# Folding a quarter of an adjacency tile onto another in TensorE, so that VectorE searches 6144 columns of a tile where it searched 8192

## The chip, the cores and the metric

The kernel runs on one core of a Trainium2 chip. The metric is device time in microseconds (us), the median of the runs. The engines are named as the profile names them: PE is TensorE (PEld its weight loads), DVE is VectorE, ACT is ScalarE, POOL is GpSimd, SP is SyncE, which here only issues DMAs.

## The reference, cut to what matters

One layer of graph attention over 8192 nodes with 256 features, 8 heads of 32, and a dense 8192 x 8192 adjacency matrix `adj` of which few entries are not zero: the probability of an entry falls with both its row and its column number, so the first rows and the first columns are the fullest (738 in the fullest row, and at most twenty in each of the last).

```python
h = relu(layernorm(x))
hw = (h @ W.T).reshape(n, H, D)                  # H = 8, D = 32
attn = s_src[:, None, :] + s_dst[None, :, :]     # s_src, s_dst: hw against a_src, a_dst
attn = attn + adj[:, :, None] * We[:, 0] + be
attn = where(adj[:, :, None] > 0, attn, -inf)
attn = softmax(leaky_relu(attn, 0.2), axis=1)
out = x + einsum('ijh,jhd->ihd', attn, hw) + h @ Wr.T + br
```

## The kernel before

Each row's few neighbours are found, their rows of a table are gathered, and attention is computed over the gathered rows alone.

The head (to 285 us) projects all nodes and writes a table of 8192 rows of 264 numbers (256 features, 8 scores) to DRAM; beside it the very full rows of tile 0 are searched in four "windows".

The loop has two streams. The first is the search. A tile is 128 rows of `adj`, 8192 columns, 4 MB. SP loads it in eight pieces of 1024 columns into one of two buffers (`adj_sb`); a piece of the tile after next waits until DVE has passed those columns (semaphore `scanned`). DVE cuts the columns into segments (the table `SEGS`: 35 for tile 1, 7 from tile 48 and 32 on) and takes from each segment the eight largest values of every row (`v.max`, L757) and their columns (`v.max_index`, L746), in `scan`. `keys` packs value and column into two words, `sort_step` sorts these with `max` and `match_replace`, `decode` writes a list of the K nearest columns and values of each row. If a segment holds eight or more entries in a row, the tile is flagged and would be computed densely at the end; so is one whose list is too short.

Tiles come in ten groups. When all tiles of a group are found, its rows are ranked by their number of neighbours, dealt to units by rank (POOL writes each row's list to its place in DRAM, `deal`, L625, and loads them back, `load_dealt`, L637), so that a unit is 128 rows with at most K neighbours. There are 67 units, K from 75 down to 7, and 1262 gathers in all.

The second stream is the units. For each, POOL issues K indirect DMAs (`gather`, L600), one for each neighbour number, into a ring of 86 slots; a gather waits until the gather four issues before it has landed (four lanes) and until PE has summed what stood in its slot. ACT prepares the scores, DVE does the softmax (L883 to L894), ACT the exponentials (L1166), DVE weights three fifths of the gathered rows (L904), ACT the rest (L1172), PE sums them in PSUM by matmuls with an identity (`tile_sums`, L1304 and L1310), and DVE scales the sum in the next unit (`evacuate`, L917). After the gathers of unit u, POOL stores unit u-4 by an indirect DMA (`store`, L616), which waits for that `evacuate`.

What sets the order: every engine has one program in order. DVE does in unit u the finds that the table `FOUND` gives it (19 in units 1 to 11, then one for each unit to unit 45, then 7 until unit 60), and the last of them is interleaved with the unit's softmax. PE has only `tile_sums` and a few small matmuls for ranks. The four windows' results are combined on DVE in units 60 to 63 and added to the output by POOL in unit 65 (L648).

## Time and profile before

| what | value |
|---|---|
| median of 3 runs | 2366.17 us (2361.86 to 2367.48) |
| the profiled execution | 2366.95 us, of which the trace spans 2365.2 |
| DVE busy | 2042.5 us, 86% |
| POOL busy | 1607.2 us, 68% |
| ACT busy | 1080.1 us, 46% |
| PE busy | 1011.7 us, 43%, mean granted clock 0.68 |

A busy share counts the time in which an engine executes. An engine that issues DMAs spends time around them too, which stands as idle time "ended by issue"; so POOL's 68% has to be read with the idle time in front of its instructions and with what ended it. Of the chain that ended last the page shows only the last DMA; who bounds the loop has to be read from the waits.

### The profile page before, as it was taken

The page shows a single profiled execution, that of the slowest core. Times are in us where ns is not written, and L with a number is a line of the kernel's source. Part 1 is how long each engine was busy: PE and PEld are TensorE (multiplying, and loading weights), DVE is VectorE, ACT ScalarE, POOL GpSimd, SP SyncE. Part 2 cuts the span into 40 slices and gives each one's busy share as a digit, 9 for nine tenths or more (in the row PEclk, how much of TensorE's full clock was granted, in tenths as well). Part 3 has the DMA queues.
Part 4 walks back from the last instruction along what each step waited for, and adds up shares of the span by engine and source line. Part 5 has one row for each costly group of instructions (what it writes and reads, how often), then busy time and mean ns, then how long its engine had stood idle before and what let it go on. Part 6 is the DMA issues. An engine that isn't in the chain of part 4 may idle for free. (4 is left out here: it accounts for less than half of the span.)

```text
span 2365.2 us, 22833 instructions
## 1 busy us (share of the span) xinstructions
PE 1011.7 (43%) x3773; PEld 798.4 (34%) x3774; DVE 2042.5 (86%) x5463; ACT 1080.1 (46%) x4646; POOL 1607.2 (68%) x1939
## 2 busy tenths in 40 slices
PE   4766304422453274336333543362344336353344
PEld 3555203322432153325322433252234225242232
DVE  4899798899699679998988899999999998888733
ACT  2333206532574264446544645453453446475454
POOL 5444476667676677667777777677677775677775
PEclk9988656666765566666666766676666666677676
DMA  6444876677676867787777688788888886777443
GB/s 145 158 144 139 298 211 167 196 232 229 138 210 216 233 165 223 233 247 213 238 230 227 190 254 254 236 244 255 254 259 245 258 263 189 207 215 207 99 89 67
DMA packets 167080, 489.46 MB, mean 207 GB/s; under 512 B 35888, under 2 KB 54360, under 8 KB 166728
## 3 DMA queue, kind: packets, MB, share of 16 engines
q1 hardware_dynamic: 86088, 278.11, 36.0%
q0 software_dynamic: 80848, 209.94, 34.5%
q14 instruction: 116, 0.95, 0.1%
q8 instruction: 28, 0.46, 0.1%
HBM read 451.08 MB, written 36.83 MB: 206 GB/s over the span
## 5 line engine op out<-in xcount | busy, mean ns | idle before, releaser
L600 POOL DMA_INDIRECT arena<-table,arena x1262 | 1285.7, 1019 | 504.3 <-issue 316.3
L1304 PE MATMUL banks<-arena,ident 128*128 128x264 f32 x1566 | 501.8, 493 | 1206.3 <-DVE arena L904 1206.3
L1304 PEld LDWEIGHTS banks<-arena,ident 128*128 128x128 f32 x1566 | 386.2, 252 | 1319.0 <-issue 1092.4
L1172 ACT ACTIVATE arena<-arena 128x32 f32<-128x32 f32 x3832 | 819.3, 306 | 2.2
L746 DVE FIND_INDEX8 work<-work,adj_sb 128x8 uint32<-128x502 f32 (+56 forms) x775 | 667.0, 865 | 0.0
L757 DVE MAX8 work<-adj_sb 128x8 f32<-128x502 f32 (+56 forms) x775 | 652.1, 856 | 0.0
L1166 ACT ACTIVATE arena<-pre 128x104 f32<-128x104 f32 (+22 forms) x81 | 23.2, 302 | 998.2 <-DVE pre L894 998.2
L1310 PE MATMUL banks<-arena,ident 128*128 128x264 f32 x958 | 253.8, 407 | 39.2 <-ACT arena L1172 38.8
L904 DVE TENSOR_TENSOR arena<-arena 128x1024 f32<-128x1024 f32 (+8 forms) x169 | 226.3, 1388 | 37.4 <-ACT arena L1166 37.3
L1310 PEld LDWEIGHTS banks<-arena,ident 128*128 128x128 f32 x958 | 181.7, 196 | 99.4 <-ACT arena L1172 71.9
L1156 ACT ACTIVATE pre<-arena,we_all 128x13 f32<-128x13 f32 (+26 forms) x536 | 165.2, 406 | 87.7 <-DMA arena<-lists 87.7
L883 DVE TENSOR_TENSOR pre<-pre,arena 128x104 f32<-128x104 f32 (+22 forms) x81 | 21.5, 280 | 187.6 <-DMA arena<-table,arena 76.4
L806 DVE MAX8 work<-work 128x8 f32<-128x56 f32 (+11 forms) x580 | 132.9, 270 | 2.3
L808 DVE MATCH_REPLACE8 work<-work 128x56 f32<-128x56 f32 (+11 forms) x446 | 118.3, 272 | 0.2 <-issue 0.2
L616 POOL DMA_INDIRECT out_dram<-w_all,arena x41 | 66.7, 1626 | 47.1 <-DVE w_all L917 23.4
L1114 ACT ACTIVATE arena<-arena 128x256 f32<-128x256 f32 x64 | 29.0, 500 | 146.5 <-DVE arena L712 146.4
L625 POOL DMA_INDIRECT lists<-arena,rank x67 | 66.9, 999 | 36.5 <-issue 21.3
L1280 PE MATMUL banks<-w_all,arena 128*128 128x272 f32 x256 | 83.5, 455 | 1.9 <-ACT arena L1122 1.8
L1326 PE MATMUL banks<-work,ones 128*128 128x24 f32 (+9 forms) x390 | 80.2, 356 | 0.0
L1326 PEld LDWEIGHTS banks<-work,ones 128*128 128x128 f32 x390 | 75.9, 287 | 0.0
L570 POOL TENSOR_TENSOR arena<-arena 128x512 f32<-128x512 f32 x32 | 40.4, 1263 | 48.7 <-DVE arena L727 48.5
L1283 PE MATMUL banks<-w_all,arena 128*128 128x256 f32 x256 | 72.8, 411 | 0.0
(127 smaller groups left out, 931.8 us busy)
## 6 DMA issues: line engine op xcount, KB each, us to landing
adj_sb<-in_adj_dram SPq DMA_DIRECT2D x505, 512.0 KB, 4.6
arena<-table,arena POOLq DMA_INDIRECT x1262, 4.0
table<-arena POOLq DMA_DIRECT2D x32, 264.0 KB, 2.6
arena<-in_x_dram SPq DMA_DIRECT2D x32, 256.0 KB, 2.9
resid<-arena POOLq DMA_DIRECT2D x32, 256.0 KB, 2.6
out_dram<-arena POOLq DMA_DIRECT2D x32, 256.0 KB, 2.8
adj_sb<-in_adj_dram SPq DMA_DIRECT2D x1, 1536.0 KB, 23.1
lists<-arena,rank POOLq DMA_INDIRECT x67, 3.8
```

The lines of the kernel that those rows point to most:

```text
L600: pool.indirect_dma_start(gath[:, un.slot(k), :], None, table[:, :], bass.IndirectOffsetOnAxis(ap=rec[:, k, 0:1], axis=0)).then_inc(lane, 16)
L746: v.max_index(idx8[:, 8 * s:8 * s + 8], val8[:, 8 * s:8 * s + 8], a[:, bounds[s]:bounds[s + 1]]).then_inc(S["scanned"], 1)
L757: v.max(val8[:, 8 * s:8 * s + 8], a[:, bounds[s]:bounds[s + 1]]).then_inc(S["maxed"], 1)
L806: v.max(top, keys_of).then_inc(done, 1)
L808: v.match_replace(keys_of, top, keys_of, 0.0).then_inc(done, 1)
L904: last = v.tensor_tensor(gv, gv, pb.unsqueeze(3).to_broadcast([P, n, H, D]), ALU.mult)
L1156: last = s.activation(pv[:, h, :], pairs(rec, K)[:, :, 1], ACT.Identity, scale=we_all[:, h:h + 1], bias=rec[:, 1 + h:2 + h])
L1172: last = s.activation(g, g, ACT.Copy, scale=gath[:, un.slot(k), HD + h:HD + h + 1])
L1280: m.matmul(ps_hd[:, q, b, :], rows, w_all[:, c, 0:272], start=(c == 0), stop=(c == 1))
L1304: last = m.matmul(ps_sum[:, u % 2, :], ident[:, :], gath[:, un.slot(k), :], start=(k == 0), stop=False)
L1310: last = m.matmul(ps_sum[:, u % 2, :], ident[:, :], gath[:, un.slot(k), :], start=False, stop=(k == K - 1))
L1326: m.matmul(rv[:, i, :], ones[:, :], same[:, j * D:(j + 1) * D], start=False, stop=(i == n - 1 and j == i - 1))
```

## The change

From tile 5 on (59 of 63 tiles) PE adds, for four banks of PSUM of 512 columns each, columns 4096 to 6143 of the tile (times an identity) and columns 6144 to 8191 (times an identity scaled by 2^-64). A bank holds then both halves: what stands near keeps its size (0.05 to 1), what stands far is below 2^-32. DVE searches the four banks as four segments and columns 0 to 4095 in 5 to 11 more. `unfold` then marks the small values, adds the distance to their column and multiplies them by 2^64. Two entries of one row that fall on the same folded column, or eight of a row in a bank, would flag the tile; the table `TURNS` turns the far banks against the near ones, tile by tile. To tell a collision, ACT counts the entries of both halves (two `Sign` activations of 2048 columns with an accumulator, `see_fold`), DVE counts those found, and `fold_flags` compares the counts at the end. The pieces of a folded tile are loaded upper half first, and the upper half's buffer is free when ACT has counted it (`fold_seen`). The table `SEGS` is another, and `FOUND` ends the finds at unit 57 where it was 60.

The diff, cut to its core (semaphore names, bases of the segments and buffers are left out; of the tables the lines that the text speaks of stand):

```diff
+FOLD_FROM = 5
+FOLD_SCALE = 2.0 ** -64
-FOUND = ((0, 7), (11, 26), (45, 60), (60, 67))
+FOUND = ((0, 7), (11, 26), (45, 60), (57, 67))
...
-                for n in range(PIECES):
+                for i, n in enumerate(so.pieces):
                     cols = slice(n * PIECE, (n + 1) * PIECE)
-                    lane = S[f"adj_in{b}{n % 2}"]
-                    sp.wait_ge(S["scanned"], segs_before[c - 2] + scans_of(sources[c - 2], n))
+                    lane = S[f"adj_in{b}{i % 2}"]
+                    if sources[c - 2].folded and n * PIECE >= FOLD_AT:
+                        sp.wait_ge(S["fold_seen"], sources[c - 2].fold + 1)
+                    else:
+                        sp.wait_ge(S["scanned"], segs_before[c - 2] + scans_of(sources[c - 2], n))
...
+                def segment(s):
+                    if s < so.banks:
+                        return ps_fold[:, s, :]
+                    return a[:, bounds[s - so.banks]:bounds[s - so.banks + 1]]
...
+                    elif s < so.banks:
+                        dve.wait_ge(S["folded"], BANKS * so.fold + s + 1)
...
+            def unfold(so):
+                f = so.fold
+                vf, jf = val8[:, 0:8 * BANKS], jpad[:, 0:8 * BANKS]
+                v.tensor_scalar(fold_tag[:, :], vf, FOLD_SPLIT, 1.0 / FOLD_SCALE, ALU.is_lt, ALU.mult
+                                ).then_inc(S["tagged"], 1)
+                v.tensor_scalar(fold_one[:, 0, :], vf, FOLD_SPLIT, 0.0, ALU.is_ge, ALU.add,
+                                accum_out=fold_found[:, 0, f:f + 1])
+                v.tensor_scalar(fold_one[:, 1, :], vf, 0.0, 0.0, ALU.is_gt, ALU.add,
+                                accum_out=fold_found[:, 1, f:f + 1])
+                dve.wait_ge(S["jshift"], so.c + 1)
+                dve.wait_ge(S["tagged"], f + 1)
+                cut = 8 * (BANKS - so.turn)
+                for lo, hi, far in ((0, cut, FOLD + BANK * so.turn), (cut, 8 * BANKS, BANK * so.turn)):
+                    if hi > lo:
+                        last = v.scalar_tensor_tensor(out=jf[:, lo:hi], in0=fold_tag[:, lo:hi],
+                                                      scalar=float(far << JBITS) * FOLD_SCALE, in1=jf[:, lo:hi],
+                                                      op0=ALU.mult, op1=ALU.add)
+                v.scalar_tensor_tensor(out=vf, in0=fold_tag[:, :], scalar=1.0, in1=vf, op0=ALU.max, op1=ALU.mult
+                                       ).then_inc(S["unfolded"], 1)
+                dve.wait_ge(S["unfolded"], f + 1)
...
+            def see_fold(so):
+                act.wait_ge(S["folded"], BANKS * (so.fold + 1))
+                for side in range(2):
+                    cols = adj_sb[:, so.buf, FOLD_AT + FOLD * side:FOLD_AT + FOLD * (side + 1)]
+                    last = s.activation(cols, cols, ACT.Sign, bias=tiny[:, :],
+                                        accum_out=fold_counts[:, side, so.fold:so.fold + 1])
+                last.then_inc(S["fold_seen"], 1)
...
+                while seen < found[un.u]:
+                    if sources[seen].folded:
+                        see_fold(sources[seen])
+                    seen += 1
                 exps(un)
...
+            def fold(so):
+                before = sources[so.c - 1]
+                for q in range(BANKS):
+                    near, far = FOLD_AT + BANK * q, FOLD_AT + FOLD + BANK * ((q + so.turn) % BANKS)
+                    adj_landed(pe, so, near, near + BANK)
+                    adj_landed(pe, so, far, far + BANK)
+                    if before.folded:
+                        pe.wait_ge(S["scanned"], segs_before[before.c] + q + 1)
+                    m.matmul(ps_fold[:, q, :], ident[:, :], adj_sb[:, so.buf, near:near + BANK], start=True, stop=False)
+                    m.matmul(ps_fold[:, q, :], small_ident[:, :], adj_sb[:, so.buf, far:far + BANK], start=False, stop=True
+                             ).then_inc(S["folded"], 1)
...
             for un in units:
+                while folds < min(len(sources), found[un.u] + 1):
+                    if sources[folds].folded:
+                        fold(sources[folds])
+                    folds += 1
                 tile_sums(un)
```

DVE, the end of the search of one late tile and its keys, in the kernel before (`flag` and the 128x56 words are the seven segments' results):

```order
L746 MAX_INDEX work<-work,adj_sb 128x8
L757 MAX work<-adj_sb 128x8
L746 MAX_INDEX work<-work,adj_sb 128x8 x3
L769 TENSOR_REDUCE flag<-work 128x1
L772 SCALAR_TENSOR_TENSOR work<-work,seg_base_20 128x56
L776 SCALAR_TENSOR_TENSOR work<-work 128x56
L780 SCALAR_TENSOR_TENSOR work<-work 128x56
L782 SCALAR_TENSOR_TENSOR work<-work 128x56
```

The same place on DVE in the changed kernel, whose nine segments are four banks and five pieces of the lower half:

```order
L800 MAX work<-adj_sb 128x8
L791 MAX_INDEX work<-work,adj_sb 128x8 x3
L857 TENSOR_REDUCE flag<-work 128x1
L860 SCALAR_TENSOR_TENSOR work<-work,seg_base_5_17 128x72
L811 TENSOR_SCALAR fold_tag<-work 128x32
L813 TENSOR_SCALAR fold_one,fold_found<-work 128x32
L815 TENSOR_SCALAR fold_one,fold_found<-work 128x32
L822 SCALAR_TENSOR_TENSOR work<-fold_tag,work 128x32
L825 SCALAR_TENSOR_TENSOR work<-fold_tag,work 128x32
L866 SCALAR_TENSOR_TENSOR work<-work 128x72
L870 SCALAR_TENSOR_TENSOR work<-work 128x72
L872 SCALAR_TENSOR_TENSOR work<-work 128x72
```

Five instructions of 32 columns stand between the first and the second instruction on the keys, and the words are 72 wide where they were 56.

PE, the sums of three units (K of 18, 17 and 15) in the kernel before, where `ident` is the identity and `banks` is PSUM:

```order
L1304 MATMUL banks<-arena,ident 128x264 x11
L1310 MATMUL banks<-arena,ident 128x264 x7
L1304 MATMUL banks<-arena,ident 128x264 x11
L1310 MATMUL banks<-arena,ident 128x264 x6
L1304 MATMUL banks<-arena,ident 128x264 x9
L1310 MATMUL banks<-arena,ident 128x264 x6
```

PE at the first two of these in the changed kernel, with the fold of one tile between them:

```order
L1411 MATMUL banks<-arena,ident 128x264 x11
L1417 MATMUL banks<-arena,ident 128x264 x7
L1447 MATMUL banks<-adj_sb,ident 128x512
L1448 MATMUL banks<-adj_sb,small_ident 128x512
L1447 MATMUL banks<-adj_sb,ident 128x512
L1448 MATMUL banks<-adj_sb,small_ident 128x512
L1447 MATMUL banks<-adj_sb,ident 128x512
L1448 MATMUL banks<-adj_sb,small_ident 128x512
L1447 MATMUL banks<-adj_sb,ident 128x512
L1448 MATMUL banks<-adj_sb,small_ident 128x512
L1411 MATMUL banks<-arena,ident 128x264 x11
L1417 MATMUL banks<-arena,ident 128x264 x6
```

Eight matmuls of 512 columns have come in front of each unit's sums; they are those of the tile that is searched one unit later.

POOL, the end of the program in the kernel before, with the deal (`lists`) and the load (`arena<-lists`) of the last group:

```order
L600 DMA arena<-table,arena 128x264 x11
L616 DMA out_dram<-w_all,arena 8192x256
L600 DMA arena<-table,arena 128x264 x9
L616 DMA out_dram<-w_all,arena 8192x256
L600 DMA arena<-table,arena 128x264 x8
L616 DMA out_dram<-more_out,arena 8192x256
L625 DMA lists<-arena,rank 512x45 x4
L637 DMA arena<-lists 128x4x45
L600 DMA arena<-table,arena 128x264 x18
```

The same units on POOL in the changed kernel (L686 adds the windows' combined result):

```order
L638 DMA arena<-table,arena 128x264 x11
L654 DMA out_dram<-w_all,arena 8192x256
L663 DMA lists<-arena,rank 512x45 x4
L638 DMA arena<-table,arena 128x264 x9
L654 DMA out_dram<-w_all,arena 8192x256
L675 DMA arena<-lists 128x4x45
L638 DMA arena<-table,arena 128x264 x8
L654 DMA out_dram<-more_out,arena 8192x256
L686 DMA out_dram<-adj_sb 128x256
L638 DMA arena<-table,arena 128x264 x18
```

The deal stands two units earlier and the load one unit earlier; between the deal, the load and the gathers that use them there are now other gathers. The gathers and stores are the same ones in the same order.

## Rows read from the trace of the kernel before

**Rows 1.** Page, part 1: busy us (share of the span) xinstructions

```profile
PE 1011.7 (43%) x3773; PEld 798.4 (34%) x3774; DVE 2042.5 (86%) x5463; ACT 1080.1 (46%) x4646; POOL 1607.2 (68%) x1939
```

**Rows 2.** Groups by line, POOL: busy us, mean ns | idle us before <-who ended it

```profile
L600 POOL DMA_INDIRECT arena<-table,arena x1262 | 1285.7, 1019 | 504.3 <-issue 316.3 <-DMA arena<-table,arena 134.7 <-DMA arena<-lists 27.5
...
L616 POOL DMA_INDIRECT out_dram<-w_all,arena x41 | 66.7, 1626 | 47.1 <-DVE w_all L917 23.4 <-DMA arena<-table,arena 20.0 <-issue 3.7
...
L543 POOL MEMSET seg_base<- 128x8 f32 x155 | 5.4, 95 | 0.0
```

**Rows 3.** Waits, all engines: engine line <- whom: us, times, longest us

```profile
DVE pre L883 <- DMA arena<-table,arena: 76.4, 14, 11.5
...
POOL arena L600 <- PE banks L1304: 1.8, 3, 1.2
```

**Rows 4.** POOL's timeline, its first gather: start us, us, instruction [idle before <-who]

```profile
284.88 1.01 POOL L600 DMA_INDIRECT arena<-table,arena  x1 [7.59 <-DMA arena<-lists]
```

**Rows 5.** POOL's timeline around unit 48's end

```profile
1979.19 0.95 POOL L600 DMA_INDIRECT arena<-table,arena  x1 [0.30 <-issue]
1994.22 1.62 POOL L616 DMA_INDIRECT out_dram<-w_all,arena  x1 [14.08 <-DVE w_all L917]
```

**Rows 6.** POOL's timeline at the last group's lists

```profile
2264.76 0.81 POOL L637 DMA_DIRECT2D arena<-lists  x1 [1.51 <-DMA lists<-arena,rank]
2268.07 1.00 POOL L600 DMA_INDIRECT arena<-table,arena  x1 [2.51 <-DMA arena<-lists]
```

**Rows 7.** Timeline of all engines at the end

```profile
2340.23 0.22 DVE L883 TENSOR_TENSOR pre<-pre,arena 128x56 f32<-128x56 f32 x1 [7.98 <-DMA arena<-table,arena]
...
2342.38 4.72 PE L1304 MATMUL banks<-arena,ident 128*128 128x264 f32 x10 [4.40 <-DVE arena L904]
...
2349.07 1.56 POOL L616 DMA_INDIRECT out_dram<-w_all,arena  x1 [3.46 <-DVE w_all L917]
```

**Rows 8.** Waits of POOL from 400 to 1000 us

```profile
POOL arena L600 <- DMA arena<-table,arena: 51.7, 81, 2.5
```

**Rows 9.** Waits of POOL from 1400 to 2000 us

```profile
POOL arena L600 <- DMA arena<-table,arena: 37.3, 59, 1.7
POOL out_dram L616 <- DVE w_all L917: 20.0, 2, 14.1
```

**Rows 10.** Waits of POOL from 2000 us to the end

```profile
POOL arena L600 <- DMA arena<-table,arena: 9.6, 20, 1.5
```

**Rows 11.** Stretches: busy us of each engine, granted clock, DMA share, GB/s

```profile
600.00:800.00 200.00, 91.71 (x324) 66.48 (x324) 177.41 (x480) 118.28 (x541) 138.62 (x135) 0.67 0.69 199
1600.00:1800.00 200.00, 83.81 (x298) 68.35 (x298) 197.74 (x425) 89.76 (x393) 144.49 (x141) 0.64 0.83 256
```

**Rows 12.** Groups by line and shape, DVE's search and sort

```profile
L746 DVE FIND_INDEX8 work<-work,adj_sb 128x8 uint32<-128x2173 f32 x16 | 38.6, 2415 | 0.0
...
L806 DVE MAX8 work<-work 128x8 f32<-128x56 f32 x192 | 31.8, 206 | 1.1
...
L806 DVE MAX8 work<-work 128x8 f32<-128x72 f32 x128 | 23.3, 223 | 0.5
...
L746 DVE FIND_INDEX8 work<-work,adj_sb 128x8 uint32<-128x502 f32 x16 | 10.8, 675 | 0.0
```

**Rows 13.** DVE's timeline, the key words of one tile

```profile
1604.78 0.22 DVE L780 SCALAR_TENSOR_TENSOR work<-work 128x56 uint32<-128x56 uint32 x1
1604.91 0.21 DVE L782 SCALAR_TENSOR_TENSOR work<-work 128x56 uint32<-128x56 uint32 x1
```

**Rows 14.** Groups by line, DVE, two from SBUF alone and with PSUM

```profile
L847 DVE TENSOR_TENSOR work<-degree,work 128x192 f32<-128x192 f32 (+9 forms) x11 | 4.0, 361 | 0.4
...
L859 DVE TENSOR_TENSOR work<-work,banks 128x192 f32<-128x192 f32 (+9 forms) x11 | 3.8, 348 | 3.4 <-PE banks L1328 3.4
```

**Rows 15.** Groups by line, ACT

```profile
L1172 ACT ACTIVATE arena<-arena 128x32 f32<-128x32 f32 x3832 | 819.3, 306 | 2.2
...
L1114 ACT ACTIVATE arena<-arena 128x256 f32<-128x256 f32 x64 | 29.0, 500 | 146.5 <-DVE arena L712 146.4
```

More of the change, by code:

```diff
@@ L102, in __init__, with base, places @@
             self.shape = SEGS[max(a for a in SEGS if a <= t)]
-            self.bounds, self.exact = segments(*self.shape), 0
+            self.bounds, self.exact = segments(*self.shape, FOLD_AT if t >= FOLD_FROM else N), 0
             self.buf, self.col = c % 2, 0
-        self.segs = len(self.bounds) - 1
+        self.folded = t is not None and t >= FOLD_FROM
+        self.banks = BANKS if self.folded else 0
+        self.turn = TURNS[t - FOLD_FROM] if self.folded else 0
+        self.fold = t - FOLD_FROM if self.folded else None
+        self.segs = self.banks + len(self.bounds) - 1
+        self.pieces = [(n + (PIECES // 2 if self.folded else 0)) % PIECES for n in range(PIECES)]
+    def base(self):
+        return [FOLD_AT + BANK * q for q in range(self.banks)] + list(self.bounds[:-1])
+    def places(self, cols):
+        return [i for i, n in enumerate(self.pieces) if cols[0] < (n + 1) * PIECE and cols[1] > n * PIECE]
     def windows(self):
@@ L198, in plan, with segments @@
     return sources, units, groups, found, issued
-def segments(n, power):
+def segments(n, power, width):
     bounds = [0]
     for s in range(1, n + 1):
-        bounds.append(max(bounds[-1] + 8, int(round(N * (s / n) ** power))))
+        bounds.append(max(bounds[-1] + 8, int(round(width * (s / n) ** power))))
     return bounds
@@ L237, in gat_kernel @@
         ps_out = banks[:, 4:6, 256:256 + D]
+        ps_fold = banks[:, 4:4 + BANKS, :]
         ps_rank, ps_above = banks[:, 2, :], banks[:, 3, :]
@@ L247, in gat_kernel @@
         we_all = sb("we_all", [P, H])
-        seg_base = {(n, w): sb(f"seg_base{n}_{int(10 * w)}", [P, n * 8]) for n, w in sorted(set(SEGS.values()))}
+        seg_base = {(f, n, w): sb(f"seg_base{f}_{n}_{int(10 * w)}", [P, (f + n) * 8])
+                    for f, n, w in sorted({(so.banks,) + so.shape for so in sources[NV:]})}
         s_all = sb("s_all", [P, TILES, H])
@@ L422, in scans_of, with adj_landed @@
         def scans_of(so, n):
-            return sum(lo < (n + 1) * PIECE for lo in so.bounds[:-1])
+            return so.banks + sum(lo < (n + 1) * PIECE for lo in so.bounds[:-1])
+        def adj_landed(eng, so, *cols):
+            for i in so.places(cols)[-2:]:
+                eng.wait_ge(S[f"adj_in{so.buf}{i % 2}"], 16 * (loads_before(so) * (PIECES // 2) + i // 2 + 1))
         def loads_before(so):
@@ L539, in _ @@
             pool.memset(adj_sb[:, 0, :], 0.0).then_inc(S["window_zero"], 1)
-            for (n, power), base in seg_base.items():
-                bounds = segments(n, power)
-                for s in range(n):
-                    last = pool.memset(base[:, 8 * s:8 * s + 8], float((bounds[s] + PAD) << JBITS))
+            for shape, base in seg_base.items():
+                so = next(so for so in sources[NV:] if (so.banks,) + so.shape == shape)
+                for s, at in enumerate(so.base()):
+                    last = pool.memset(base[:, 8 * s:8 * s + 8], float((at + PAD) << JBITS))
             for so in sources[:NV]:
@@ L751, in scan @@
                         dve.wait_ge(S[f"window_in{c}"], 16 * sum(1 for _ in so.windows()))
-                    else:
-                        pieces, before = -(-bounds[s + 1] // PIECE), loads_before(so)
-                        for lane in range(2):
-                            if pieces > lane:
-                                dve.wait_ge(S[f"adj_in{b}{lane}"], 16 * (before * (PIECES // 2) + (pieces - lane + 1) // 2))
-                    v.max(val8[:, 8 * s:8 * s + 8], a[:, bounds[s]:bounds[s + 1]]).then_inc(S["maxed"], 1)
+                    elif s < so.banks:
+                        dve.wait_ge(S["folded"], BANKS * so.fold + s + 1)
+                    else:
+                        adj_landed(dve, so, 0, bounds[s - so.banks + 1])
+                    v.max(val8[:, 8 * s:8 * s + 8], segment(s)).then_inc(S["maxed"], 1)
                     if s >= 2:
@@ L774, in keys @@
                                        ).then_inc(S["jshift"], 1)
+                if so.folded:
+                    unfold(so)
                 dve.wait_ge(S["jshift"], c + 1)
```

63 lines of the change are left out of this document (54 added, 9 removed).

## The prediction

> **What bounds the kernel now.** The page's busy shares come first [rows 1]: DVE 86%, POOL 68%, ACT 46%. By these DVE is the bound, and the change takes work from DVE. The waits say otherwise, so I read them second, POOL's first.
>
> POOL's gathers are one instruction group [rows 2]: 1262 of them, 1285.7 us busy and 504.3 us idle in front of them, together 1790.0 us. They begin at 284.88 us [rows 4]. The timeline shows how one costs: 0.95 us of execution and 0.30 us in front of it that waits for nobody [rows 5], so 1.25 us each even when everything is there. Of the 504.3 us idle, "issue" holds 316.3, the landing of earlier gathers 134.7, lists 27.5 [rows 2]; the wait for a ring slot, that is for PE's sums, is 1.8 us in the whole run [rows 3]. Add the stores, deals and loads on the same queue, and POOL is occupied from 285 us to the end with next to no wait for another compute engine. The exception is the store of unit u-4, which waited for DVE's `evacuate`: 23.4 us in all [rows 2], of which 20.0 in two waits between 1400 and 2000 us [rows 9], one of them 14.08 us long [rows 5].
>
> DVE, the busiest by the page, waits for POOL: 76.4 us for gathers in front of the softmax [rows 3]. The last unit shows the pair plainly: DVE idles 7.98 us until the gather has landed at 2340 us, and nine microseconds later all is stored but the last result [rows 7]. So the loop has two nearly equal streams. Between about 1400 and 2000 us DVE is the slower one (197.7 of 200 us busy, [rows 11]), POOL runs ahead until it hits the store, and elsewhere POOL sets the pace. Only what DVE makes POOL wait for can be won.
>
> **The change part by part.**
>
> *DVE's search.* FIND_INDEX8 takes 2415 ns for 2173 columns and 675 for 502 [rows 12], so 1.041 ns a column; MAX8 stands within 11 ns of it. 2048 columns less, searched twice: 2048 x 2 x 1.041 = 4.26 us a tile, times 59 = 251.6 us removed. The segments of all tiles rise from 624 to 700 (both tables summed over the tiles and windows). A segment's fixed part is 675 - 502 x 1.041 = 152 ns for one pass, of which the neighbours overlap some; between 0.1 and 0.3 us for both passes, I take 0.19: 76 x 0.19 = 14 us added. A late tile sorts 72 words for 56: 223 against 206 ns [rows 12], 17 ns on 15 instructions in some 32 tiles, 8 us.
>
> *`unfold`.* Five instructions, six in the 12 tiles that are turned: 307. The trace has short ones of the same kind at 0.13 us from start to start and 0.21 to 0.22 us each [rows 13]; 307 x 0.13 = 40 us to 307 x 0.25 = 77 us (the upper with a wait), I take 58. DVE's sum is -251.6 + 14 + 8 + 58 = -172 us, 8% of its busy time.
>
> PE writes the banks that DVE reads, and reading PSUM is no dearer here: 348 ns for an operation that reads PSUM against 361 for its twin from SBUF [rows 14]. The Trainium skill, "VectorE: DVE Perf Modes", section on the TRN2 errata, gives 120 cycles of fixed cost from PSUM and 58 from SBUF at 0.96 GHz; that would be an estimated 65 ns on 8 scans of 59 tiles, 30 us, and DVE's saving 142 us. The trace does not agree with it.
>
> *PE.* 8 matmuls of 512 columns a tile. Ten of 264 took 4.72 us [rows 7], 0.47 each; by columns 0.92 for 512, 7.3 us a tile and 431 us in all, bounded by nothing if all is hidden and by 7.3 us a tile if none is. A tile's fold stands one unit ahead of its search, in front of that unit's sums, which wait for DVE's weights of the same unit, after a whole search. PE is busy 84 of 200 us [rows 11]. Hidden, with slack: POOL's ring does not wait for PE [rows 3].
>
> *ACT.* 306 ns for 32 columns and 500 for 256 [rows 15] give 0.87 ns a column; 2048 columns 2.05 us, two of them 4.1 us a tile, 242 us in all. They stand in front of the unit's exponentials, which wait for DVE's search anyway; ACT is busy 90 to 118 of 200 us [rows 11]. Hidden. If that cover goes, DVE's weighting is late by up to 4.1 us a unit.
>
> *New waits.* DVE's first four scans wait for `folded`; queued behind are the softmax and `evacuate`, for which POOL's stores wait, with about a unit (20 us) to spare. SP's upper pieces wait for ACT's count and not for DVE's scan, so they come as a burst of four; the gathers on POOL meet them on the way.
>
> *Where it reaches the end.* The two store waits of 20.0 us go (but for 0.30 in front of each): -19.4. If DVE should remain slower there, nothing goes; if other POOL waits were DVE's as well, the bound is the 23.4 of [rows 2]. What is late next is POOL itself, gather after gather. The last group's deal moves two units up and its load one, past other gathers: its waits of 1.51 and 2.51 us [rows 6] fall to 0.30 each, -3.4, or stay. The head gets 49 more small memsets on POOL (204 for 155), whose 155 took 5.4 us [rows 2]: +1.7 on DVE's start. The earlier end of the finds (unit 57) only moves DVE's work.
>
> *The landing waits.* 134.7 us over 2055 us of loop is 0.066 a microsecond. From 400 to 1000 us it is 51.7/600 = 0.086 [rows 8], from 2000 us on, with the finds thinning out, 9.6/366 = 0.026 [rows 10]. At the one rate throughout the loop they would be 177 us (+42), at the other 54 (-81). The bytes are the same and the time nearly so; I take 0, since the rate between 1400 and 2000 us, 37.3/600 = 0.062 [rows 9], is no higher although the DMA share is (0.83 against 0.69, [rows 11]).
>
> Sum: 2366.95 - 19.4 - 3.4 + 1.7 = 2345.9 us for the profiled execution, which is 0.8 above the median shown; so 2345 us.
>
> **The rivals.**
>
> *DVE is the bound after all.* Then its whole 172 us come out: 2366 - 172 = 2194 us. For it: 86% busy, and near 99% from 1600 to 1800 us. Against it: POOL's gathers alone, at 1.25 us, are 1578 us, and POOL waits for DVE only 23 us. A part of it, 40 us or more gained, would need the landing waits to fall as well.
>
> *Nothing moves.* The 20 us come back as landing waits elsewhere, since POOL is then one steady stream and its DMA lanes never rest: 2360 to 2371 us. For it: in [rows 8] each such wait is 0.64 us (51.7 in 81), and 33 more of them are enough.
>
> *The loads collide with the gathers (slower).* The place is the four lanes of POOL in units 1 to 45, where every find issues four upper pieces at once and ACT's count, not DVE's scan, sets their moment. If the landing waits rise by more than 21 us, 16% of 134.7, the gain is gone. At the highest rate of the rows the time is 2345 + 42 = 2387 us; with the waits doubled, 2345 + 135 = 2480. Against it: the rate does not follow the DMA share. The Trainium skill, "Trainium Kernel Development and Optimization", Key Constraints, says that DMAs issued by SP, ACT and POOL run on the same 16 DMA engines and interleave; by that a burst must lengthen the gathers beside it, and what it adds would have to come back when the queue is empty.
>
> *The search waits for its fold (slower).* In units with two finds the second tile's fold stands behind the sums of the unit before, and these end with ACT's share of the weighting (K of 20 to 75). If 15 us a unit showed in 11 units, 165 us, and POOL's lead hid half, the time would be some 2345 + 80 = 2425 us.
>
> *The change doesn't do what it says*: a collision of two entries would flag a tile and bring the dense path. With these inputs the folded banks hold at most 7 entries in a row and no two on one column, worked out from the reference's inputs; no chance.
>
> **How the numbers follow.** Forecast (20 us gained, between 8 and 60) 0.55; DVE the bound, wholly or in part, over 60 us gained, 0.09; nothing moves 0.18; loads collide 0.13; the search waits 0.05. A difference under 0.3% (7 us) can't be told from none. Faster 0.55 + 0.09 = 0.64, same 0.18, slower 0.18. The range of 8 in 10 runs from 2300 us, which takes in landing waits 45 us shorter (half of that bound), to 2390 us, the collision at the highest rate of the rows.
>
> **What would show it.** DVE about 1870 us busy, its wait in front of the softmax up by some 150 us, POOL's store waits for DVE gone, POOL's gathers as before at 1.25 us from start to start, PE up by 430 us, ACT by 240, no wait of 0.5 us or more for `folded`. I am wrong if POOL's landing waits differ by more than 20 us from 134.7, if the ring makes POOL wait for PE, or if gathers get shorter than 0.95 us.

## The result and the profile after

The changed kernel takes 2379.33 us (median of 4 runs, 2376.05 to 2380.1) against 2365.95 for the kernel before in the same comparison: a ratio of 1.0058 (95% interval 1.0043 to 1.0073). It is slower by 13.4 us where 20 us less was forecast. The profiled execution has a span of 2377.9 us and a time of 2379.56 us.

The work came and went as it was meant to. The page's first part, busy us of each engine, against [rows 1]:

```profile
PE 1435.4 (60%) x4717; PEld 982.6 (41%) x4718; DVE 1865.6 (78%) x6123; ACT 1314.5 (55%) x4882; POOL 1606.0 (68%) x1989
```

DVE has 176.9 us less, PE 423.7 more, ACT 234.4 more, and POOL, which sets the pace, is unchanged. So the time must be in POOL's pauses. Its groups by line (busy us, mean ns | idle us before, and who ended it), against [rows 2]:

```profile
L638 POOL DMA_INDIRECT arena<-table,arena x1262 | 1281.9, 1016 | 547.5 <-issue 299.0 <-DMA arena<-table,arena 191.5 <-DMA arena<-lists 17.0
...
L654 POOL DMA_INDIRECT out_dram<-w_all,arena x41 | 66.4, 1619 | 21.1 <-DMA arena<-table,arena 10.9 <-issue 5.4 <-DVE w_all L1007 4.1
```

The idle time before the stores fell from 47.1 to 21.1 us, and DVE's part in it from 23.4 to 4.1: the forecast's gain is there. But the idle time before the gathers rose from 504.3 to 547.5 us, and within it the waits for landings from 134.7 to 191.5. (Each such wait contains the 0.30 us that stands before every gather, and "issue" shrank by 17.3 us as more gathers waited; so the net price is the 43.2 us.) From the first gather to the last is 2066.3 us, 13.3 more than before; that is the whole result. Counted from the records over this whole stretch, each wait less the 0.30 us that stands before every DMA on this queue: POOL's waits for landings of its own transfers (gathers, stores, deals) rose from 117 to 160 us, its waits for DVE fell from 19 to 0, its waits for lists from 24 to 13. That is +43 - 19 - 11 = +13 us. The head is no part of it: the first gather starts 1.5 us earlier than in [rows 4].

```profile
283.37 1.01 POOL L638 DMA_INDIRECT arena<-table,arena  x1 [4.68 <-DMA arena<-lists]
```

By stage, POOL's waits from 400 to 1000, 1400 to 2000 and 2000 us on, in this order, against 51.7, 37.3 and 9.6 in [rows 8 to 10]:

```profile
POOL arena L638 <- DMA arena<-table,arena: 59.6, 73, 2.7
```
```profile
POOL arena L638 <- DMA arena<-table,arena: 57.5, 79, 2.5
```
```profile
POOL arena L638 <- DMA arena<-table,arena: 23.4, 35, 1.9
...
POOL out_dram L654 <- DVE w_all L1007: 4.1, 1, 4.1
```

The rise is largest in the stretch that held the two store waits, 20 us; from 2000 us on, where the finds thin out, it is still 14. The only wait of a store for DVE that is left there is that of the last unit. POOL's timeline shows how a landing wait looks: the second gather here needs the lane of the one four before it, and that had not landed for another 2.02 us.

```profile
1618.06 0.95 POOL L638 DMA_INDIRECT arena<-table,arena  x1 [0.30 <-issue]
1621.02 0.95 POOL L638 DMA_INDIRECT arena<-table,arena  x1 [2.02 <-DMA arena<-table,arena]
```

DVE now waits for POOL, in front of the softmax 179.2 us against 76.4 in [rows 3]; and its search waits for the fold:

```profile
DVE pre L973 <- DMA arena<-table,arena: 179.2, 23, 16.8
DVE pre L973 <- DMA part_ml<-ml,arena: 76.8, 2, 51.6
...
DVE work L800 <- PE banks L1448: 47.8, 32, 17.8
```

What released the loads has changed too. SP's waits, first in the kernel before, then after (L486 and L523 issue a tile's pieces, L485 and L522 wait for the piece two before):

```profile
SPq L486 <- DVE work L746: 1135.9, 277, 47.4
SPq L485 <- DMA adj_sb<-in_adj_dram: 608.3, 344, 7.0
```
```profile
SPq L522 <- DMA adj_sb<-in_adj_dram: 904.2, 378, 7.1
SPq L523 <- ACT adj_sb L1272: 720.9, 49, 104.3
...
SPq L523 <- DVE work L791: 91.8, 28, 32.8
```

Before, 277 waits for DVE's scan metered the pieces out one by one. Now SP waits 49 times, about once a tile, for ACT's count, 28 times for DVE, and else for its own landings: from the count on, the pieces go out nearly as fast as the two lanes take them. A load is in flight from its issue until it has landed. Counted from the records of all loads, two or more were in flight for 42% of the gather loop before and 55% after, exactly one for 29% and 8%. From the records of gathers, the mean time from the end of the issuing instruction to the landing is 2.05 us beside no load, 3.0 before and 2.8 after beside one, and 4.0 beside two in both kernels; beside three, which only the changed kernel has (24 gathers), it is 5.5. Three more gathers at 1.25 us and the 0.30 us give some 4.05 us before a lane is wanted again, so two loads are the point at which four lanes begin not to suffice.

### The profile page after: what moved, and what is told of

The parts are those of the page before. It is cut to its first block and busy times, and to the rows that moved or that the text cites. A ratio compares the mean times of both kernels' runs of the same rounds, so it can differ in the third digit from the quotient of the medians.

```text
span 2377.9 us, 25865 instructions
## 1 busy us (share of the span) xinstructions
PE 1435.4 (60%) x4717; PEld 982.6 (41%) x4718; DVE 1865.6 (78%) x6123; ACT 1314.5 (55%) x4882; POOL 1606.0 (68%) x1989
## 5 line engine op out<-in xcount | busy, mean ns | idle before, releaser
L638 POOL DMA_INDIRECT arena<-table,arena x1262 | 1281.9, 1016 | 547.5 <-issue 299.0
L791 DVE FIND_INDEX8 work<-work,adj_sb 128x8 uint32<-128x266 f32 (+44 forms) x615 | 392.4, 644 | 0.0
L800 DVE MAX8 work<-adj_sb 128x8 f32<-128x266 f32 (+44 forms) x615 | 388.2, 633 | 0.0
L1447 PE MATMUL banks<-adj_sb,ident 128*128 128x512 f32 x472 | 266.9, 649 | 101.4 <-DMA adj_sb<-in_adj_dram 93.0
L973 DVE TENSOR_TENSOR pre<-pre,arena 128x104 f32<-128x104 f32 (+22 forms) x81 | 21.9, 284 | 363.6 <-DMA arena<-table,arena 179.2
L1448 PE MATMUL banks<-adj_sb,small_ident 128*128 128x512 f32 x472 | 256.1, 626 | 0.0
L1272 ACT ACTIVATE adj_sb<-adj_sb,tiny 128x2048 f32<-128x2048 f32 x118 | 234.4, 1987 | 31.3 <-PE banks L1448 31.3
L800 DVE MAX8 work<-banks 128x8 f32<-128x512 f32 x236 | 153.5, 686 | 47.9 <-PE banks L1448 47.8
L791 DVE FIND_INDEX8 work<-work,banks 128x8 uint32<-128x512 f32 x236 | 163.0, 691 | 0.0
L1448 PEld LDWEIGHTS banks<-adj_sb,small_ident 128*128 128x128 f32 x472 | 96.6, 205 | 127.4 <-issue 127.4
L896 DVE MAX8 work<-work 128x8 f32<-128x72 f32 (+14 forms) x580 | 136.7, 277 | 2.3
L898 DVE MATCH_REPLACE8 work<-work 128x72 f32<-128x72 f32 (+14 forms) x446 | 120.6, 278 | 0.0
```

The lines of the kernel that those rows point to most:

```text
L638: pool.indirect_dma_start(gath[:, un.slot(k), :], None, table[:, :], bass.IndirectOffsetOnAxis(ap=rec[:, k, 0:1], axis=0)).then_inc(lane, 16)
L791: v.max_index(idx8[:, 8 * s:8 * s + 8], val8[:, 8 * s:8 * s + 8], segment(s)).then_inc(S["scanned"], 1)
L800: v.max(val8[:, 8 * s:8 * s + 8], segment(s)).then_inc(S["maxed"], 1)
L896: v.max(top, keys_of).then_inc(done, 1)
L1272: last = s.activation(cols, cols, ACT.Sign, bias=tiny[:, :], accum_out=fold_counts[:, side, so.fold:so.fold + 1])
L1447: m.matmul(ps_fold[:, q, :], ident[:, :], adj_sb[:, so.buf, near:near + BANK], start=True, stop=False)
```

## The experiments

Each ratio is to the kernel before, run beside it; the changed kernel's is 1.0058. "Landing" is POOL's wait of gathers for gathers (134.7 us before, 191.5 after). "Lanes" is the count from above over all of POOL's waits for landings of its own transfers in the gather loop, each less 0.30 us (117 before, 160 after). The edits below are cut to the lines that matter, and shortened within the line.

| run | time us | ratio, 95% interval | landing us | lanes us | DVE busy us |
|---|---|---|---|---|---|
| e2 count early | 2392.24 | 1.0109 [1.0082, 1.0135] | 195.9 | 169 | 1862 |
| e3 after, 6 lanes | 2278.63 | 0.9641 [0.9616, 0.9666] | 51.4 | 24 | 1863 |
| e4 before, 6 lanes | 2316.08 | 0.9789 [0.9768, 0.9811] | 52.5 | 27 | 2046 |
| e5 before, less search | 2381.85 | 1.0086 [1.0066, 1.0106] | 161.6 | 148 | 1852 |
| e6 before, bunched | 2369.72 | 1.0044 [1.0025, 1.0063] | 160.7 | 145 | 2044 |
| e7 after, half pieces | 2350.59 | 0.9954 [0.9935, 0.9972] | 99.4 | 70 | 1873 |
| e8 after, 8 lanes | 2219.40 | 0.9402 [0.9384, 0.9420] | 32.6 | 4 | 1867 |
| e9 before, 8 lanes | 2312.88 | 0.9779 [0.9763, 0.9796] | 40.7 | 16 | 2048 |
| e10 before, e5 + e6 | 2402.57 | 1.0148 [1.0123, 1.0172] | 177.2 | 172 | 1853 |
| e11 after, more search | 2386.23 | 1.0082 [1.0064, 1.0101] | 188.3 | 162 | 2035 |
| e12 after, small count | 2394.93 | 1.0115 [1.0083, 1.0148] | 192.7 | 174 | 1864 |
| e13 after, spread | 2390.78 | 1.0110 [1.0081, 1.0139] | 198.7 | 165 | 1865 |
| e14 after, spread, more search | 2383.37 | 1.0081 [1.0052, 1.0110] | 172.6 | 156 | 2034 |
| e15 after, paced by the scan | 2365.72 | 1.0014 [0.9994, 1.0034] | 179.8 | 147 | 1864 |
| e16 = e15, more search | 2364.26 | 1.0002 [0.9985, 1.0020] | 175.6 | 136 | 2035 |

### Half of the change, in the kernel before

**e1, a shorter search (no verdict).** The segments of tiles 8 and on span 6656 columns instead of 8192.

```
-self.bounds = segments(*self.shape)
+self.bounds = segments(*self.shape, N if t < 8 else SHORT)
```

> The kernel before, with DVE searching only columns 0 to 6655 of each tile from tile 8 on (56 tiles; all 8192 columns are still loaded, the output lacks the neighbours left out). DVE loses about 2 x 1536 x 1.041 ns x 56 = 179 us of work, as the change does (177 us measured), with no fold on PE, no count on ACT and the loads released by DVE's scan as before. Theory A (the change's late and bunched release of the loads lengthens the gathers): the 20 us of store waits go, POOL's landing waits stay near 135 us, 2345 us (ratio 0.991). Theory B (POOL without pauses takes back in landing waits whatever DVE gives): landing waits 155 us or more, 2366 us or above.

It took 9399 us: rescaled segments hold eight entries of a row, tiles are flagged, and the dense path runs (PE has 16,125 matmuls instead of 3773). It says nothing of the question; e5 takes its place.

**e5, a shorter search.** The segments stay as they are and are clipped at 6656 columns, from tile 5 on; the entries beyond are left out.

```
+self.bounds = clipped(segments(*self.shape), N if t < 5 else SHORT)
```

> The kernel before, with DVE searching only columns 0 to 6655 from tile 5 on, its segments cut off there (all columns are still loaded; the neighbours in the last 1536 columns are left out, the 1262 gathers stay). DVE loses 2 x 1536 x 1.041 ns x 59 = 189 us of work; PE, ACT and the rule by which DVE's scan releases the loads are as before. Theory A (what lengthens the gathers is how the change bunches its loads): store waits gone, landing waits near 135 us, 2340 to 2350 us. Theory B (any time that DVE gives back is lost again in landing waits): landing waits 155 us or more and 2360 us or above.

DVE lost 190 us, the stores' waits for DVE went, as in the changed kernel, and the kernel became slower by 0.9%, as theory B had it. Its gathers' row shows where:

```profile
L606 POOL DMA_INDIRECT arena<-table,arena x1262 | 1287.5, 1020 | 524.0 <-issue 307.1 <-DMA arena<-table,arena 161.6 <-DMA arena<-lists 21.5
```

Not quite "all loads as before": the last two pieces, beyond the clip, are now released together, so there is some bunching in it (two or more loads in flight for 48% of the loop instead of 42%, one for 20% instead of 29%).

**e6, the loads in a bunch.** All eight pieces of a tile wait for the whole scan of the tile two back.

```
-sp.wait_ge(S["scanned"], segs_before[c - 2] + scans_of(sources[c - 2], n))
+sp.wait_ge(S["scanned"], segs_before[c - 2] + sources[c - 2].segs)
```

> The kernel before, with all eight pieces of a tile released together when DVE has passed the whole tile before last, and nothing else changed. Theory A: two loads are in flight for more of the loop, landing waits rise from 135 us to 170 to 200, and the time to 2385 to 2410 us. Theory B: DVE works as before, so landing waits and time stay (2366 us), unless DVE has to wait for columns, which the trace would show in front of its MAX8.

With DVE's work unchanged (2044 us) the landing waits rise by 26 us and the time by 0.4%; two or more loads are in flight for 55% of the loop. The sign is theory A's, the size is not: it expected 170 us or more of landing waits and 2385 us or more. POOL, slower by its lanes, also waits less for DVE at the stores of `w_all` (8.5 us, 23.4 before), which pays a part of the price.

**e10, both at once.**

> The kernel before with both halves of the cause: segments clipped at 6656 columns from tile 5 on (entries beyond are left out, DVE does some 189 us less), and a tile's eight pieces released together once the tile two back is scanned. If the two causes add up, landing waits 134.7 + 27 + 26, about 188 us, and 2385 to 2400 us. If either alone makes the whole effect (both only let POOL run without pauses), about 162 us of landing waits and 2375 to 2383 us.

2402.57 us: in time the two add up (0.9 + 0.4 against 1.5%), and in the lanes nearly (31 + 28 against 56 us). In the landing waits alone they do not quite: 42.5 against 53 us.

### Taking away what the waits are made of

**e3 and e4, six gather lanes.** The same edit in the changed kernel and in the one before.

```
-LANES = 4
+LANES = 6
```

> The changed kernel with six lanes for POOL's indirect DMAs (a gather waits for the landing of the gather six before, not four). If landing waits are what the change lost its gain to, and are waits for a lane and not a full DMA queue: landing waits from 191 us to under 40, POOL's loop 2066 us less about 140, 2230 to 2260 us. If the DMA queue itself is full, gathers get longer than 1.0 us instead and the time stays within 20 us of 2379.

> The kernel before with six lanes. The landing waits of 135 us go as in the changed kernel, but DVE (2042 us busy) then sets the pace for more of the loop: store waits on DVE rise from 23 us to 60 or more, 2300 to 2330 us, so that the changed kernel with six lanes is 2 to 4% faster than this one. If the DMA queue itself is full: 2366 us.

The landing waits fall to 51 and 52 us in both, most of which is the 0.30 us that each contains (119 and 117 waits), and both kernels get faster. In e4 DVE then holds up the stores. e3 missed its expectation (under 40 us and 2230 to 2260 us), and so the change is worth 1.5% at six lanes (0.9641 / 0.9789), not 2 to 4. e3 has an odd end: its last store is issued at 2215.0 us, and what follows takes 64 us, where every other run here but e1 takes some 16; without those 48 us the change would be worth 3.7%.

**e9 and e8, eight lanes.** The same edit with 8, before and after.

> The kernel before with eight gather lanes for four. Theory B (with lanes to spare the landing waits go, and then DVE's work is what counts): as with six lanes, 2316 +- 8 us, since DVE is the bound by then; POOL's store waits for DVE stay near 65 us, gathers wait under 5 us for landings. With the changed kernel's 2219 us at eight lanes the change is then worth about 4%. Theory A (the change costs time whatever the lanes are): about 2219 / 1.006, that is 2206 us.

> The changed kernel with eight lanes for POOL's indirect DMAs. With six the waits in front of the gathers beyond 0.30 us are already down to some 45 us, of which half are for lists and stores: another 10 to 25 us less, 2255 to 2270 us, if the lanes are all that holds POOL. If the DMA queue is full, gathers get longer and the time stays at 2279 us.

The kernel before gains nothing more over six lanes; the changed one reaches 2219 us, the fastest here, and below its expectation, which was reckoned from e3 with its long end. Against each other that is 0.9402 / 0.9779 = 0.961: with lanes to spare the change is worth 3.9%. POOL's stores in e9, and then its gathers and stores in e8:

```profile
L616 POOL DMA_INDIRECT out_dram<-w_all,arena x41 | 67.3, 1641 | 76.8 <-DVE w_all L917 65.2 <-issue 10.1 <-DMA arena<-table,arena 1.5
```
```profile
L638 POOL DMA_INDIRECT arena<-table,arena x1262 | 1280.2, 1014 | 411.9 <-issue 355.4 <-DMA arena<-table,arena 32.6 <-DMA arena<-lists 11.9
L654 POOL DMA_INDIRECT out_dram<-w_all,arena x41 | 68.1, 1662 | 18.1 <-issue 10.7 <-DVE w_all L1007 6.9 <-DMA arena<-table,arena 0.6
```

411.9 us before 1262 gathers is 0.33 each, near the 0.30 of an unhindered one. In e9 the stores wait 65 us for DVE, in e8 they wait 7.

**e7, pieces of half the size.**

```
-PIECES = 8
+PIECES = 16
```

> The changed kernel with sixteen pieces of 512 columns for eight of 1024, two in flight as before, so half the bytes in flight ahead of a gather. Theory A: landing waits fall from 191 us to under 120 and the time to 2310 to 2345 us, if the loads still keep up with DVE. Theory B: landing waits stay near 190 us, 2379 us. Twice the number of load DMAs costs SP alone.

Beside two half pieces a gather lands after 3.0 us, no longer 4.0, and the landing waits halve, as theory A had it; 25 us come back by the ratios, to just above its range. But with two smaller pieces in flight a tile's load takes longer (32 us from its first issue to its last landing, 22 in the changed kernel), PE and DVE wait for it, and the stores' waits for DVE are back (56.0 us for `w_all`):

```profile
PE banks L1447 <- DMA adj_sb<-in_adj_dram: 345.5, 36, 29.9
```
```profile
POOL out_dram L654 <- DVE w_all L1007: 56.0, 6, 14.6
```

### Which half does it in the changed kernel

**e2, ACT counts a unit earlier**, so that the pieces are released earlier.

```
-while seen < found[un.u]:
+while seen < min(len(sources), found[un.u] + 1):
```

> The changed kernel, with ACT counting a tile one unit earlier (as soon as PE has folded it), so that the upper pieces of the tile after next are released a unit earlier. Theory A: two and more loads in flight for less of the time, landing waits from 191 us down to 135 to 155, 2340 to 2350 us. Theory B: landing waits stay near 190 us and the time near 2379 us. If ACT's exponentials are held up by the earlier count, the time goes up to 2390 us or more.

No cure: by the ratios 12 us slower than the changed kernel, as the last clause of the expectation had it. Three or more loads were in flight for 9% of the loop (3% after), and ACT stood waiting for the fold, its exponentials behind it:

```profile
ACT adj_sb L1272 <- PE banks L1448: 443.1, 56, 24.9
```

**e11, DVE as busy as before.** The last segment's MAX8 is repeated into a tile that nobody reads.

```
+width = bounds[-1] - bounds[-2]
+for r in range(round(2780 / width) if so.folded else 0):
+    v.max(again8[:, 8 * r:8 * r + 8], segment(so.segs - 1))
```

> The changed kernel with about 2780 columns of MAX8 a folded tile added on DVE (results unused), some 2.9 us a tile, 170 us in all: DVE is as busy as before the change. Theory B (DVE's spare time only turned into landing waits): no slower than the changed kernel, 2360 to 2380 us, landing waits down from 191 to 150 to 175, store waits on DVE back at 10 to 40 us. Rival (DVE's work is on the path in the changed kernel as well): 2400 us or more, up to 2379 + 170.

My theory half missed: 170 us more on DVE cost little (1.0082 against 1.0058, intervals that overlap), as it said, but the landing waits stayed at 188 and the stores did not wait for DVE again. So in the changed kernel the waits don't come from DVE's spare time.

**e12, ACT's count cut to 8 columns a side.**

```
-last = s.activation(cols, cols, ACT.Sign, bias=tiny[:, :],
+last = s.activation(cols[:, 0:8], cols[:, 0:8], ACT.Sign, bias=tiny[:, :],
```

> The changed kernel in which ACT counts 8 columns a side instead of 2048 (the check of the fold for collisions is left out); SP's upper pieces still wait for this count. ACT does some 235 us less. If ACT's work is hidden, as the prediction had it: 2379 +- 8 us, landing waits 191 +- 15. Rival (the length of the count sets when upper pieces are released, and so the bunching): pieces go out 4 us earlier, landing waits differ by more than 20 us and the time by more than 10 us.

200 us less of ACT's work bought nothing, so it is off the path. That it was slower than the changed kernel, by 14 us as the ratios have it, fits neither expectation well; its landing waits are those of the changed kernel (192.7), while other waits of POOL grew (for its lanes in all 174 us, 160 after). Its runs scatter from 2375 to 2402 us.

**e13 and e14, loads spread by an added wait** for DVE's scan, the wait for ACT's count left in place; e14 with e11's repeated search.

```
+sp.wait_ge(S["scanned"], segs_before[c - 2] + spread_scans(sources[c - 2], i))
 sp.wait_ge(S["fold_seen"], sources[c - 2].fold + 1)
```

> The changed kernel; a tile's eight loads are let go one after another, each when a further eighth of the searched columns of the tile two back is scanned, as they were before the change. DVE's work stays short. If bunching costs in the changed kernel what it cost in the kernel before (26 us of landing waits, 10 us of time): landing waits 191 -> 160 to 175, 2365 to 2375 us. If bunching is all of the loss: landing waits near 135 and 2340 to 2355 us, what the prediction expected. If only DVE's shorter work counts: 2379 +- 6.

> As e13, and DVE's work made as long as before by the repeated MAX8 of e11 (170 us, results unused). Both causes undone at once: landing waits 135 to 150, store waits on DVE back at 20 to 60 us, 2358 to 2372 us. If a third thing in the change holds POOL up (ACT's count, PE's folds), it shows here: landing waits stay above 170, or 2380 us and more.

Neither says what it was made to say, because the edit didn't spread the loads. e13's SP still waits for ACT, and by the time the count comes the scan is done (rows below). So e13 is a measure of something else: an edit that leaves the loads as they were moved the ratio from 1.0058 to 1.0110, with intervals apart.

```profile
SPq L532 <- DMA adj_sb<-in_adj_dram: 902.2, 373, 8.7
SPq L528 <- ACT adj_sb L1282: 714.4, 47, 102.9
```

**e15 and e16, loads paced by the scan alone.** ACT reads one word elsewhere instead of the tile (the count is left out), so SP needs to wait for PE's fold and DVE's scan only; e16 with e11's repeated search.

```
-sp.wait_ge(S["fold_seen"], sources[c - 2].fold + 1)
+sp.wait_ge(S["folded"], BANKS * (sources[c - 2].fold + 1))
-last = s.activation(cols, cols, ACT.Sign, bias=tiny[:, :], accum_out=...)
+last = s.activation(fold_counts[:, side, so.fold:so.fold + 1], tiny[:, :], ACT.Sign, bias=tiny[:, :])
```

> The changed kernel without ACT's count (the check of the fold for collisions is left out), so that SP needn't wait for ACT: a tile's eight loads are let go one by one as DVE scans the tile two back, an eighth of the columns each, as before the change; DVE's work is as short as in the changed kernel. In e13 SP still waited 714 us for the count and the loads stayed bunched; here they can't. If ACT's late release and the burst behind it are the loss: 2340 to 2360 us, landing waits 135 to 155. If DVE's shorter work is the loss, as in e5: 2375 to 2390 us, landing waits 160 or more.

> As e15, with DVE's work made as long as before the change by the repeated MAX8 of e11. If the two causes of e5 and e6 are all there is, both are gone: 2355 to 2372 us, landing waits 130 to 150, store waits on DVE 15 to 60 us. If PE's folds or the rest of the change hold POOL up: 2378 us or more.

e15's SP is metered by DVE again:

```profile
SPq L533 <- DVE work L801: 796.9, 221, 72.0
SPq L532 <- DMA adj_sb<-in_adj_dram: 777.7, 363, 6.1
```

and the loss is gone: 1.0014 against 1.0058. After e13, two intervals that are apart don't carry this alone. But the five kernels that ACT's count releases at its first place (the changed one, e11, e12, e13, e14) stand at 1.0058 to 1.0115, and the two that the scan paces at 1.0014 and 1.0002. e15 against e12, which also has next to no count but the old release, is 24 us by the ratios; e16 against e11 and e14, with the same longer search, 19 us. Making DVE 170 us longer (e16) changes nothing that can be told from e15. e15's time is in neither of its expected ranges, and in both runs the landing waits are above the 155 and 150 us expected if the release was all. The gathers' rows of e15 and e16:

```profile
L648 POOL DMA_INDIRECT arena<-table,arena x1262 | 1285.0, 1018 | 539.5 <-issue 303.9 <-DMA arena<-table,arena 179.8 <-DMA arena<-lists 25.8
```
```profile
L649 POOL DMA_INDIRECT arena<-table,arena x1262 | 1281.6, 1016 | 530.1 <-issue 308.0 <-DMA arena<-table,arena 175.6 <-DMA arena<-lists 20.1
```

Even here landing waits are 41 to 45 us above the kernel before, at its time. Over all lanes e16 waits 136 us and 4 for DVE, where the kernel before waits 117 and 19: the stores' waits for DVE come back as waits for landings. That is what the rival "nothing moves" said. (e15's 147 us are from an execution of 2373 us, one of the slower of its twelve.) How much of this is POOL's steadier pace is not separated from bunching that is left: two or more loads are in flight for 51% of the loop in e15 and 48% in e16, between the 42% before and the 55% after. So of the change at four lanes, DVE's saved time is worth nothing that shows, and the new release of the loads makes the larger part of the loss or all of it (10 of 14 us by the changed kernel and e15, 19 to 24 us by the pairs).

## Why the prediction was wrong

**What bounds the kernel: right.** POOL sets the pace, DVE's 177 us were not the path: with DVE made as long again (e11, e16) the time hardly moves. What I did not see is that POOL's pace at four lanes is set by its landings.

**The terms of the work: right in size, PE's by luck.** DVE -176.9 for -172, PE +423.7 for +431, ACT +234.4 for +242. Their rows in the page (busy us, mean ns | idle us before):

```profile
L1447 PE MATMUL banks<-adj_sb,ident 128*128 128x512 f32 x472 | 266.9, 649 | 101.4 <-DMA adj_sb<-in_adj_dram 93.0
...
L1448 PE MATMUL banks<-adj_sb,small_ident 128*128 128x512 f32 x472 | 256.1, 626 | 0.0
L1272 ACT ACTIVATE adj_sb<-adj_sb,tiny 128x2048 f32<-128x2048 f32 x118 | 234.4, 1987 | 31.3 <-PE banks L1448 31.3
...
L800 DVE MAX8 work<-banks 128x8 f32<-128x512 f32 x236 | 153.5, 686 | 47.9 <-PE banks L1448 47.8
...
L791 DVE FIND_INDEX8 work<-work,banks 128x8 uint32<-128x512 f32 x236 | 163.0, 691 | 0.0
```

ACT's count takes 1.99 us for the 2.05 worked out. A search of 512 columns in PSUM takes 686 and 691 ns; FIND_INDEX8 from SBUF at 1.041 ns a column beyond the 675 for 502 [rows 12] would be 685, and MAX8 within 11 ns of that; so the estimated 65 ns that I left out of the sum aren't there. PE's sum is right by two errors: each matmul of the program stands in the trace as two instructions, 944 in all and not 472 (and so did the ten of [rows 7], which are five matmuls), and they cost 0.48 us each (PE is busy with them for 454 us by the records, and 20 us less with the rest), not 0.92: about the 0.47 of an instruction of 264 columns in [rows 7], though at a higher granted clock. The two stretches show it at 0.77 and 0.80, 0.67 and 0.64 in [rows 11], with PE 1.4 and 1.7 times as busy:

```profile
600.00:800.00 200.00, 128.85 (x404) 82.66 (x404) 149.13 (x469) 138.76 (x562) 137.20 (x137) 0.77 0.62 178
1600.00:1800.00 200.00, 145.35 (x457) 94.23 (x456) 187.72 (x552) 126.24 (x432) 138.47 (x136) 0.80 0.83 261
```

**The store waits: right; lists and head: small, and off.** The two waits of 20.0 us between 1400 and 2000 us are gone, -19 for -19.4. The waits for lists fell by 11 us in all, for 3.4; the head, put at +1.7, came out at -1.5.

**The search waits for its fold: it does, and it is hidden.** I said no wait of 0.5 us or more; DVE waits 32 times, 47.8 us in all, one of them 17.8. DVE has the time, and in e8, with POOL unhindered, the change still gains.

**The landing waits: the step that failed.** I took 0 between bounds of -81 and +42; they rose by 56.8 us, and over all lanes, less 0.30 us each, by 43: above my bound, by the second count barely, and twice what the store waits gave. The reason for the 0 was that the wait rate did not follow the share of busy DMA engines. That share was the wrong column: a gather's landing goes with the number of loads in flight when it is issued (2.05 us beside none, about 3 beside one, 4.0 beside two; 3.0 beside two of half the size in e7), and this the change altered, while bytes and share nearly stayed. The same "burst of four" stands in my list of new waits, and in the sum I priced it at nothing because of that column. Why the rate between 1400 and 2000 us was as low as 0.062 is not shown. Two or more loads were in flight for 54% of that stretch, against 40% from 400 to 1000 us, so their number alone does not foretell a stretch's waits. POOL stood at stores for 20 us there, but from 1000 to 1400 us, where no store waited for DVE, the rate was lower still:

```profile
POOL arena L600 <- DMA arena<-table,arena: 22.5, 35, 2.5
```

That is 0.056 a microsecond. After the change it is 0.10 in all three stretches up to 2000 us (39.9 us in this one).

**The rivals.** Two of them are true together. "Nothing moves", with a chance of 0.18, is what e15 and e16 show: the 20 us at the stores come back as landing waits. "The loads collide" is the remaining loss: its place (ACT's count releases the pieces), its sign and its condition (over 21 us) held, and its 2387 us is 8 over the measured time, in part by luck: the landing waits rose by 57 us and not by its 42, of which 17 us are idle time that stood under "issue" before. It had a chance of 0.13. The rule on shared DMA engines that I set beside it, from the Trainium skill, "Trainium Kernel Development and Optimization", Key Constraints, agrees with the landing times beside loads. What I had drawn from it, that whatever a burst adds comes back when the queue is empty, does not show: in e6 the same bytes in a bunch cost time. "DVE is the bound after all" is true with eight lanes: 94 us of its 177 show between e9 and e8.

**What stays open.** e5 in the kernel before lost 20 us with a shorter search; e15 in the changed kernel lost next to nothing. The last two pieces of e5 were bunched, which e6 prices for all eight at 10 us; this covers a part. Why e12 and e13 are slower than the changed kernel by 12 to 14 us, when the releases of the loads are the same, stays open too, and with it what differences of half a per cent between single runs here mean.

## What to carry to other kernels

Where a queue is limited by a few lanes with one transfer each, look at the landing time of a transfer against the number of transfers beside it, and compare it with the time until its lane is wanted again; the share of busy DMA engines did not tell it here. Before moving work off an engine, ask what its waits have been metering: here DVE's scan let the loads out one by one, and handing the release to another engine's single count bunched them. Add lanes first (e9, 2.2%), then the freed engine pays (e8, 3.9% more).

## What the runs showed of the hardware

- POOL's gathers take 0.95 us, but 91 of those in the kernel before took over 1.2, 81 us over the 0.945 in all; 87 of the 91 ran beside DVE's two-input TENSOR_TENSOR on line L904, beside which 144 gathers ran. Of 621 gathers beside a MAX8 of the search, 8 were long, and those touched an L904 as well. This is a coincidence in time, not tested by a run.
- After the last store e3 has an end of 64 us, e8 one of 16, and only the number of lanes differs. The instruction queue moved 160 packets in e3, 128 in e8, and 116 to 133 in the other runs, whose ends (e1's dense path apart) are 16 us too:

```profile
q14 instruction: 160, 1.31, 0.2%
```
```profile
q14 instruction: 128, 1.05, 0.1%
```

  ACT's empty loop over the flag groups took some 8 us a turn in e3 and 1.2 in e8. That code was fetched there is a reading of these packets, not a test; with an end like e8's, e3 would be near 2231 us.
